# Decoder kernel in fp32: K and V products in three reduced-precision passes, a new order of the side work, and an output projection begun in the last head group

## Chip, cores and metric

The kernel runs on one core of a Trainium2 chip. The metric is device time in microseconds (us), median of several runs; lower is better.

## What is computed

There are three residual blocks on `x` of shape (16, 224, 512), each behind a layer norm; all arrays are float32. Cut to what matters:

```python
# 1 mixer: Q, K, products with V_b, W_b, ..., a running sum over the 224 tokens, @ Wo.T
# 2 attention over ctx (16, 750, 256), 16 heads of 32
Q  = (ln(x) @ Wq.T).reshape(B, 224, 16, 32)
KV = (ctx @ Wkv.T).reshape(B, 750, 2, 16, 32)       # Wkv is (1024, 256)
x  = x + softmax(Q K^T * 32**-0.5) V @ Wo.T
# 3 router and 32 experts
probs  = softmax(ln(x) @ gate_w.T + gate_b, over the tokens)
vals, idx = top 8 tokens of each expert
merged = sum_k vals[k] * ln(x)[idx[k]]              # one row of 512 per batch and expert
o = gelu([merged, 1] @ w1[e]) ...; o = [h, 1] @ w2[e]   # w1, w2: 256 MB in all
x = x + scatter of o * vals
```

## The kernel before

**Stages.** A setup loads and transposes the weights. A main stage does mixer, attention and router of the 16 batch elements in turn. A last stage runs all 32 experts, whose 128 weight chunks of 2 MB stream through `ring`, eight slots of SBUF; it ends with the scatter. The first eight chunks are loaded during the last batch element, into space that the main stage no longer needs (`first_weights`, L647).

**Main stage.** The 16 heads are four groups `kt` of four. TensorE makes the scores twice. `scores` (L1261, matmul at L1272) makes them with the queries on partitions, only to get each query's maximum: 16 matmuls of 375 columns a group into banks 2 to 4, each reduced by VectorE (`take_max`, L1072). `join_maxima` (L1079), a transpose on TensorE (`turn_max`, L1279), `max_rows` on VectorE (L1089, L1092) and two DMAs of ScalarE's queue (`stack_max`, L906) put the negated maxima into two rows of `q_st`. Then `scores_T` (L1282, matmul at L1294) makes the scores with the keys on partitions, with the maxima subtracted, in 12 units of 2x224 columns; ScalarE takes `exp` of each (L886). `values` (L1311) multiplies with V a third of the keys at a time; GpSimd sums the probabilities (`sum_keys`, L760 to L767, 896 columns an instruction), `denominators` (L1322) sums that over partitions, and `normalise` on VectorE (L1100 to L1108) divides. The maxima of group n+1 are made during group n.

**Precision.** Both kinds of scores are made of float32r operands, split into a high and a low part that stand under each other on the partitions (`k_hi`, `k_lo`, `q_hi`, `q_lo`, stacked by 24 DMAs a group on SyncE's queue). All other matmuls, those for K (L1223), V (L1230) and the output projection (L1236) among them, are float32.

**The order of the work** is written out by hand. A group has 16 steps. Each engine walks through the same steps: in step 1 to 12 one unit of `scores_T` and its `exp`; in `PV_AT` the first two `values`, in step 1 of the next group the third; `MAXIMA` says how many maxima each step makes for the next group; `TURN_AT` the step of `join_maxima`, with the transpose and the rows one step later. `TIMETABLE` lays the other products ("jobs", function `fill` on each engine) of the next and of the past batch element into the steps: `ct0` to `ct3` transpose the context, `k0.0` to `k3.1` and `v0` to `v5` make K and V, `q0` to `q3` Q, `xt`, `pz`, `pc`, `pa`, `mix` the mixer, `yt` the transposed input of attention, `out0`, `out1` the output projection of the past element, `rt`, `gate`, `wt`, `merge`, `mt` the router. A job writes bank 0 or 1, in turn, and waits until the job two before it is read out. `AT` places the norms and the parts of the router's softmax. SyncE loads `x` and the context of the next element at the start of a batch element (`load_x`) and behind the first stack (`load_ctx`), and ScalarE may overwrite `k_hi` when the last stack of K has been copied out.

**The tail.** Behind the last group come the last `values`, `denominators`, `normalise`, `out0`, `out1`, the store of `x2`, the router's jobs, and then the barrier ahead of the experts. `mt` (L1044) writes the merged rows into `merged_T`, which is held from the start with one column for each element.

## Time and profile before

| | |
|---|---|
| median of 3 runs | 2317.16 us (2315.62 to 2319.82) |
| the profiled execution | 2323.09 us, its span 2321.4 us |
| granted TensorE clock, mean | 0.919 |
| busy in the span | TensorE 83%, VectorE 42%, GpSimd 36%, ScalarE 32% |
| transfers of the whole | 419.34 MB |

The span falls into setup (to 43.5 us), a prologue that fills the pipeline (to about 105 us), 16 batch elements (to about 1607 us), the tail (to 1640 us) and the experts with the scatter. In the rows an instruction's "mean ns" goes from its start to its modelled end; matmuls overlap, so the distance from one start to the next is shorter. A float32 matmul of the code is two records.

### The profile page before, as it was taken

To read this page: it belongs to the slowest core of one execution; us is meant where nothing else is said; L and a number is where in the kernel's file an instruction comes from. 1 tells how busy PE (TensorE), PEld (TensorE's weight loads), DVE (VectorE), ACT (ScalarE), POOL (GpSimd) and SP (SyncE) were. 2 spreads that over 40 slices of the span, in tenths; PEclk is the share of its full clock that TensorE was granted. 3 is DMA by queue.
4 is the path that set the end of the run, shared out by engine and by line. 5 is a ranking of instruction groups with operands and counts; after the bars stand their busy time and mean duration, and the time that the engine had idled before them with its cause. 6 is when DMAs were issued, how large, how long until landed. Compare 5 with 4: busy or idle time off the path is not lost. (4 is left out here: it accounts for less than half of the span.)

```text
span 2321.4 us, 40341 instructions
## 1 busy us (share of the span) xinstructions
PE 1931.5 (83%) x12130; PEld 1138.9 (49%) x12130; DVE 974.4 (42%) x2473; ACT 748.8 (32%) x1551; POOL 827.3 (36%) x592
## 2 busy tenths in 40 slices
PE   7789999999999999999999999997665556655544
PEld 5466666666666666666666666653211111111111
DVE  1355655656656556565565665653100000000003
ACT  3243444435444344344443544432100000000000
POOL 0255554545555455555455555544000000000000
PEclk9999999999999999999999999997877777777777
DMA  6224223243242332423324223255699999999996
GB/s 179 71 68 105 61 75 90 74 102 71 68 98 76 87 86 68 97 70 78 89 74 104 66 71 95 76 169 203 247 419 422 420 420 421 421 421 421 421 377 244
DMA packets 139167, 419.34 MB, mean 181 GB/s; under 512 B 32780, under 2 KB 74988, under 8 KB 114556
## 3 DMA queue, kind: packets, MB, share of 16 engines
q1 hardware_dynamic: 131484, 409.73, 51.8%
q10 hardware_dynamic: 6656, 8.15, 1.0%
q0 software_dynamic: 992, 1.02, 0.1%
q8 instruction: 19, 0.31, 0.1%
q14 instruction: 16, 0.13, 0.0%
HBM read 306.39 MB, written 16.15 MB: 139 GB/s over the span
## 5 line engine op out<-in xcount | busy, mean ns | idle before, releaser
L1072 DVE TENSOR_REDUCE maxes<-bank 112x1 f32<-112x376 f32 (+1 forms) x1024 | 506.7, 538 | 204.7 <-PE bank L1272 203.9
L886 ACT ACTIVATE probs<-bank 125x448 f32<-125x448 f32 x768 | 402.7, 547 | 369.0 <-PE bank L1294 362.4
L1294 PE MATMUL bank<-q_st,k_st 98*125 98x224 f32 x1536 | 384.0, 339 | 21.5 <-DMA q_st<-max_lo 10.3
L764 POOL TENSOR_TENSOR psum_keys<-psum_keys,probs 125x896 f32<-125x896 f32 x128 | 269.1, 2102 | 327.8 <-ACT probs L886 322.2
L1656 PE MATMUL bank<-ring,hid_T 128*32 128x512 f32 x1024 | 177.9, 857 | 199.7 <-DMA ring<-in_L_ffn_w 196.4
L1272 PE MATMUL bank<-k_st,q_st 96*112 96x376 f32 (+1 forms) x1024 | 324.0, 367 | 13.2 <-DVE maxes L1072 7.6
L1294 PEld LDWEIGHTS bank<-q_st,k_st 98*125 98x125 f32 x1536 | 265.2, 192 | 132.2 <-issue 68.8
L767 POOL TENSOR_TENSOR psum_keys<-psum_keys,probs 125x896 f32<-125x896 f32 x128 | 267.7, 2092 | 10.0
L1574 DVE TENSOR_TENSOR o_fin<-bank,b_row 16x512 f32<-16x512 f32 x32 | 21.7, 679 | 589.3 <-PE bank L1614 589.3
L1497 POOL DMA_DIRECT2D o_rows<-o_fin x31 | 15.3, 493 | 598.1 <-DVE o_fin L1574 598.1
L1629 PE MATMUL bank<-ring,tok 128*32 128x512 f32 x1024 | 145.2, 693 | 76.4 <-DMA ring<-in_L_ffn_w 74.3
L1272 PEld LDWEIGHTS bank<-k_st,q_st 96*112 96x112 f32 x1024 | 164.4, 179 | 77.6 <-DVE maxes L1072 46.8
L1656 PEld LDWEIGHTS bank<-ring,hid_T 128*32 128x32 f32 x1024 | 45.0, 150 | 308.2 <-issue 302.4
L1311 PE MATMUL bank<-probs,v 125*32 125x224 f32 x3072 | 190.1, 366 | 2.2 <-ACT probs L886 2.2
L1223 PE MATMUL bank<-ctx_T,wk_T 128*128 128x376 f32 (+1 forms) x512 | 183.2, 485 | 3.5 <-DVE q_lo L1025 2.6
L1230 PE MATMUL bank<-wv_T,ctx_T 128*125 128x512 f32 x384 | 183.4, 607 | 0.9 <-DVE q_lo L1025 0.9
L760 POOL TENSOR_TENSOR psum_keys<-probs 125x896 f32<-125x896 f32 x64 | 134.2, 2098 | 129.3 <-ACT probs L886 120.0
L1031 DVE TENSOR_TENSOR k_lo<-bank,k_hi 128x376 fp32r<-128x376 f32 (+1 forms) x128 | 69.8, 546 | 131.7 <-ACT k_hi L828 126.3
L1522 ACT COPY o_sb<-bank 128x512 f32<-128x512 f32 x32 | 18.7, 586 | 326.5 <-PE bank L1656 326.5
L724 POOL TENSOR_TENSOR rstd<-mean_var,small 112x2 f32<-112x2 f32 x48 | 9.4, 195 | 304.7 <-DVE mean_var L967 301.2
L1629 PEld LDWEIGHTS bank<-ring,tok 128*32 128x32 f32 x1024 | 33.0, 118 | 172.4 <-DMA ring<-in_L_ffn_w 103.3
L1236 PE MATMUL bank<-wo_T,o_T 128*112 128x512 f32 x256 | 115.9, 606 | 1.7 <-DVE o_T L1108 1.7
(149 smaller groups left out, 2268.6 us busy)
## 6 DMA issues: line engine op xcount, KB each, us to landing
ring<-in_L_ffn_w SPq DMA_DIRECT2D x128, 2048.0 KB, 30.5
k_st<-k_hi SPq DMA_DIRECT2D x512, 93.8 KB, 2.2
k_st<-k_lo SPq DMA_DIRECT2D x256, 93.8 KB, 2.2
q_st<-q_hi SPq DMA_DIRECT2D x504, 28.0 KB, 1.8
ctx_nat<-in_ctx SPq DMA_DIRECT2D x16, 750.0 KB
x_in<-in_x SPq DMA_DIRECT2D x16, 448.0 KB, 3.6
out<-x SPq DMA_DIRECT2D x16, 448.0 KB, 8.1
out<-ring ACTq DMA_DIRECT2D x28, 256.0 KB, 3.1
```

The source lines that it names most:

```text
L760: nc.gpsimd.tensor_tensor(psum_keys[:], lo, hi, ALU.add).then_inc(keys_summed, 1)
L764: nc.gpsimd.tensor_tensor(psum_keys[:], psum_keys[:], lo, ALU.add).then_inc(pool_chain, 1)
L767: nc.gpsimd.tensor_tensor(psum_keys[:], psum_keys[:], hi, ALU.add).then_inc(keys_summed, 1)
L886: nc.scalar.activation(probs[n % 2][:, j, :], bank[5 + u % 2][0:SK, 0:2 * T], ACT.Exp, scale=SCALE).then_inc(probs_ready, 1)
L1072: nc.vector.tensor_reduce(maxes[:, j, t, c:c + 1], bank[2 + n % 3][0:TT, 0:SC[c + 1] - SC[c]], AX.X, ALU.max).then_inc(s_drained, 1)
L1223: last = nc.tensor.matmul(ps[:, 0:SC[c + 1] - SC[c]], wk_T[:, kc, kt * P:(kt + 1) * P], ctx_T[:, kc, chunk(c)], start=(kc == 0), stop=(kc ...
L1230: last = nc.tensor.matmul(ps[0:SK, :], ctx_T[:, kc, i * SK:(i + 1) * SK], wv_T[:, kc, :], start=(kc == 0), stop=(kc == KC - 1))
L1272: nc.tensor.matmul(bank[2 + n % 3][0:TT, 0:SC[c + 1] - SC[c]], q_st[slot][0:3 * HD, j, t * TT:(t + 1) * TT], k_st[slot][0:3 * HD, j, chunk ...
L1294: last = nc.tensor.matmul(bank[5 + u % 2][0:SK, kk * T:(kk + 1) * T], k_st[slot][:, j, k * SK:(k + 1) * SK], q_st[slot][:, j, :], start=Tr ...
L1311: last = nc.tensor.matmul(bank[7][j * HD:(j + 1) * HD, 0:T], v[:, 2 * c + kk, col:col + HD], p[:, j, kk * T:(kk + 1) * T], start=(c == 0 a ...
L1629: last = nc.tensor.matmul(bank[e2][c * 32:(c + 1) * 32, :], tok[:, e2, kd, :], ring[:, slot, col:col + BANK], start=(kd == 0), stop=(kd == ...
L1656: last = nc.tensor.matmul(bank[5 + e2][c * 32:(c + 1) * 32, :], hid_T[:, e2, t, c * 32:(c + 1) * 32], ring[:, slot, col:col + D], start=(t ...
```

## The change

1. **K and V.** The weights `wk`, `wv` and the transposed context are split into float32r high and low parts: the weights once in the setup (four VectorE subtractions), the context in each `ct` job (ScalarE writes `ctx_hi`, VectorE then subtracts into `ctx_lo`). Each float32 product becomes three: high x high, high x low, low x high.
2. **All steps are laid anew**: `TIMETABLE`, `MAXIMA`, `AT`, `PV_AT`, `SUM_AT`, and `TURN_AT` goes from 11 to 13. The transposed maxima go to bank 4, which the third matmul of the next maxima uses, and the wait on `max_ready` moves from the first to the third.
3. **Loads** of `x` and context are issued one batch element earlier.
4. **Memory.** `v` shares its space with `merged_T` and the experts' first biases. So `mt` writes a small `m_now`, which is stored to DRAM for each element (`keep_routed`) and read back in the tail behind the last `values` (`recall_routed`), together with the biases.
5. **Last group of the last element.** `begin_out` puts the products of three of the four groups of `out0` and `out1` at steps 7 and 11; in the tail only the fourth is left. The last two sums of keys on GpSimd are left out, and TensorE sums that third of the keys itself (`last_denominators`).

```diff
 TIMETABLE = (
+    [(0, s, j) for s, j in ((1, "v4"), (2, "v5"), (2, "q3"), (4, "k3.0"), (5, "k3.1"),
+                              (6, "xt0"), (7, "xt1"), (8, "out0"), (9, "ct0"), (11, "out1"),
+                              (11, "ct1"), (13, "pz"), (14, "pc"), (15, "pa"))]
+    + [(1, s, j) for s, j in ((1, "ct2"), (2, "mix0"), (2, "ct3"), (4, "mix1"), (5, "k0.0"),
+                              (8, "yt0"), (9, "yt1"), (11, "q0"))]
+    + [(2, s, j) for s, j in ((0, "k0.1"), (1, "rt0"), (2, "rt1"), (5, "gate"), (10, "q1"),
+                              (12, "wt0"), (12, "wt1"), (13, "merge"))]
+    + [(3, s, j) for s, j in ((0, "k1.0"), (1, "k1.1"), (2, "mt"), (5, "q2"), (7, "v0"),
+                              (9, "v1"), (10, "k2.0"), (11, "k2.1"), (13, "v2"), (14, "v3"))]
+BEGIN_OUT = {(3, 7): "out0", (3, 11): "out1"}
-PV_AT = {6: 0, 10: 1}
+PV_AT = {6: 0, 12: 1}
-SUM_AT = {6: 0, 10: 1, 14: 2}
-TURN_AT = 11
+SUM_AT = {5: 0, 11: 1, 14: 2}
+TURN_AT = 13
-MAXIMA = ((3, 0, 3, 0, 0, 2, 2, 1, 2, 2, 1),
-          (0, 2, 1, 0, 2, 1, 3, 2, 2, 2, 1),
-          (3, 2, 0, 0, 0, 2, 2, 2, 1, 2, 2),
-          (1, 3, 1, 0, 2, 3, 0, 0, 2, 2, 2))
+MAXIMA = ((3, 3, 3, 1, 2, 2, 0, 0, 0, 1, 1),
+          (0, 1, 0, 0, 0, 3, 1, 3, 1, 2, 1, 2, 2),
+          (1, 2, 1, 0, 2, 2, 0, 2, 2, 0, 1, 1, 2),
+          (4, 0, 1, 0, 1, 2, 1, 1, 0, 2, 1, 2, 1))
...
+                def recall_routed():
+
+                    sp.wait_ge(pv_done, 12 * B)
+                    expert_biases()
+                    sp.wait_ge(m_stored, 16 * B)
+                    sp.dma_start(merged_T[:, 0:LAST].rearrange("p b k e -> p b (k e)"),
+                                 routed[0:LAST].rearrange("b p n -> p b n")
+                                 ).then_inc(routed_loaded, 16)
...
+                    elif job[:2] == "ct":
+                        kc, cols = i % 2, slice(i // 2 * 3 * SK, (i // 2 + 1) * 3 * SK)
+                        dve.wait_ge(work_full, full)
+                        dve.wait_ge(ctx_hi_ready, bb * 4 + (i + 1))
+                        nc.vector.tensor_tensor(ctx_lo[:, kc, cols], ps[:, 0:3 * SK],
+                                                ctx_hi[:, kc, cols].bitcast(F32), ALU.subtract
+                                                ).then_inc(s, 1)
...
+                        terms = [(ctx_hi, wv_hi), (ctx_hi, wv_lo), (ctx_lo, wv_hi)]
                         for kc in range(KC):
-                            last = nc.tensor.matmul(ps[0:SK, :], ctx_T[:, kc, i * SK:(i + 1) * SK],
-                                                    wv_T[:, kc, :], start=(kc == 0),
-                                                    stop=(kc == KC - 1))
+                            for n, (z, w) in enumerate(terms):
+                                last = nc.tensor.matmul(ps[0:SK, :],
+                                                        z[:, kc, i * SK:(i + 1) * SK], w[:, kc, :],
+                                                        start=(kc == 0 and n == 0),
+                                                        stop=(kc == KC - 1 and n == 2))
...
+                def last_denominators():
+
+                    p = probs[(3 * G - 1) % 2]
+                    pe.wait_ge(keys_summed, B * 12 - 1)
+                    for n in range(3):
+                        for j in range(4):
+                            part = p[:, j, (n - 1) * T:n * T] if n else psum_keys[:, j, :]
+                            last = nc.tensor.matmul(bank[7][j * HD:(j + 1) * HD, T:2 * T],
+                                                    ones[0:SK, 0:HD], part,
+                                                    start=(n == 0), stop=(n == 2))
+                    last.then_inc(den_done, 1)
+
+                def begin_out(job):
+
+                    wait_out(pe, *before(job, "tail", LAST + 1))
+                    pe.wait_ge(o_ready, LAST * 4 + (G - 1))
+                    for kt in range(G - 1):
+                        nc.tensor.matmul(bank_of(job, "tail")[0:TT, :],
+                                         tokens(o_T[:, kt, :], OUT[job][2]), wo_T[:, kt, :],
+                                         start=(kt == 0), stop=False)
```

The old `TIMETABLE` stands at L32 to L43. K's product (L1219 to L1226) is changed as V's is, with weight and context in each other's place.

## Rows read from the trace of the kernel before

**Rows 1.** The page: TensorE's busy tenths in 40 slices of 58 us
```profile
PE   7789999999999999999999999997665556655544
```
**Rows 2.** Busy time by stretch: main loop, last element, tail, experts (after POOL: clock, DMA share)
```profile
300.00:1500.00 1200.00, 1167.99 (x7662) 781.52 (x7660) 715.54 (x1799) 536.62 (x1133) 634.48 (x435) 1.00 0.33 81
1500.00:1600.00 100.00, 86.91 (x570) 53.66 (x570) 48.68 (x119) 38.47 (x82) 51.37 (x28) 0.88 0.57 194
1600.00:1640.00 40.00, 23.74 (x108) 11.39 (x105) 6.10 (x18) 7.58 (x17) 9.68 (x9) 0.67 0.22 79
1640.00:2321.00 681.00, 391.51 (x2324) 114.37 (x2324) 72.08 (x225) 57.84 (x97) 16.81 (x33) 0.78 0.97 396
```
**Rows 3.** Line 606, the context's loads: duration min/median/max, first and last start
```profile
L606 SPq DMA_DIRECT2D ctx_nat<-in_ctx x15: 285/301/482, 129.1 to 1455.0; - x15
```
**Rows 4.** Timeline of TensorE (start, us first start to last end), and single durations
```profile
L1230 PE MATMUL bank<-wv_T,ctx_T x384: 590/592/1216, 66.8 to 1529.7; 128*125 128x512 f32 x192
L1223 PE MATMUL bank<-ctx_T,wk_T x512: 475/478/611, 46.1 to 1535.8; 128*128 128x376 f32 x86, 128*128 128x374 f32 x85
...
1007.78 2.69 PE L1223 MATMUL bank<-ctx_T,wk_T 128*128 128x376 f32 x8
...
1048.47 3.60 PE L1230 MATMUL bank<-wv_T,ctx_T 128*125 128x512 f32 x8
```
**Rows 5.** The same for the float32r matmuls of both kinds of scores
```profile
L1272 PE MATMUL bank<-k_st,q_st x1024: 326/336/784, 88.2 to 1585.3; 96*112 96x376 f32 x171
...
L1294 PE MATMUL bank<-q_st,k_st x1536: 263/273/1174, 103.7 to 1605.0; 98*125 98x224 f32 x192
...
1004.07 0.51 PE L1272 MATMUL bank<-k_st,q_st 96*112 96x376 f32 x2
1004.42 0.38 PE L1294 MATMUL bank<-q_st,k_st 98*125 98x224 f32 x2
```
**Rows 6.** Groups by line: busy us, mean ns, idle before and releaser
```profile
L1072 DVE TENSOR_REDUCE maxes<-bank 112x1 f32<-112x376 f32 (+1 forms) x1024 | 506.7, 538 | 204.7 <-PE bank L1272 203.9
L1031 DVE TENSOR_TENSOR k_lo<-bank,k_hi 128x376 fp32r<-128x376 f32 (+1 forms) x128 | 69.8, 546 | 131.7 <-ACT k_hi L828 126.3 <-PE bank L1223 4.0
L828 ACT CAST k_hi<-bank 128x376 fp32r<-128x376 f32 (+1 forms) x128 | 60.4, 472 | 137.5 <-DMA k_st<-k_hi 82.7 <-PE bank L1223 50.5 <-issue 4.3
```
**Rows 7.** Timeline of all engines, from the transposed maxima to the next group's first unit
```profile
1027.17 0.26 PE L1279 MATMUL bank<-ident,q_max 112*8 112x112 f32 x1 [0.28 <-DVE q_max L1079]
...
1028.98 0.63 ACTq L906 DMA_DIRECT2D q_st<-max_lo  x1
...
1031.01 0.47 PE L1294 MATMUL bank<-q_st,k_st 98*125 98x224 f32 x2
...
1031.58 0.52 SPq L627 DMA_DIRECT2D k_st<-k_hi  x1
...
1041.72 0.48 PE L1294 MATMUL bank<-q_st,k_st 98*125 98x224 f32 x2 [0.21 <-ACT probs L886]
```
**Rows 8.** Timeline of TensorE, last groups and tail, with idle time before and releaser
```profile
1586.82 0.26 PE L1279 MATMUL bank<-ident,q_max 112*8 112x112 f32 x1
...
1593.51 1.18 PE L1294 MATMUL bank<-q_st,k_st 98*125 98x224 f32 x4 [3.52 <-DMA q_st<-max_lo]
...
1610.62 0.97 PE L1322 MATMUL bank<-psum_keys,ones 125*32 125x224 f32 x8 [2.79 <-POOL psum_keys L767]
1613.34 8.96 PE L1236 MATMUL bank<-wo_T,o_T 128*112 128x512 f32 x16 [1.74 <-DVE o_T L1108]
```
**Rows 9.** The chain that ended last, an expert pair's wait; and a group of DMA issues
```profile
1869.25 34.88 DMA ring<-in_L_ffn_w
...
x_in<-in_x SPq DMA_DIRECT2D x16, 448.0 KB, 3.6
```
**Rows 10.** Timeline of SyncE's queue in the tail
```profile
1594.31 11.49 SPq L430 DMA_DIRECT2D ring<-in_L_ffn_w  x2
1623.05 0.35 SPq L640 DMA_DIRECT2D out<-x  x1
```

More of the change, by code:

```diff
@@ L679, in step @@
                             store(b - 1)
+                        if kt == 1 and not (isint(b) and b + 2 > LAST):
+                            load_ctx(b + 2)
+                        if kt == 2 and not (isint(b) and b + 2 > LAST):
+                            load_x(b + 2)
                         if kt == 0:
@@ L683, in step @@
                             stack(b + 1, kt - 1)
[L684 to L685 removed]
                         if kt == 3 and kind != "first":
                             keep_weight(b - 1)
+                        if kt == 3 and kind != "first":
+                            keep_routed(b - 1)
                         if kind == "last" and kt == 1:
[L689 removed]
                             sp.wait_ge(x1_ready, 2 * B)
@@ L701, in step @@
                             first_weights([2 + kt])
-                batches(sp, step)
+                step("pro", -1)
+                step("first", 0)
+                with sp.Fori(1, LAST - 1) as b:
+                    step("mid", b)
+                step("mid", LAST - 1)
+                step("last", LAST)
+                step("tail", LAST + 1)
                 sp.wait_ge(x2_stored, 16 * B)
@@ L791, in step @@
                                 root(2, norm_no(2, kind, b))
-                            if s in SUM_AT:
+                            if s in SUM_AT and not (kind == "last" and (kt, SUM_AT[s]) == (3, 2)):
                                 sum_keys(b, kt, SUM_AT[s])
@@ L1176, in fill @@
                     prev = before(job, kind, b)
-                    if prev:
+                    if prev and not (kind == "tail" and job[:3] == "out"):
                         wait_out(pe, *prev)
@@ L1368, in step @@
                                     denominators(b - 1, G - 1)
+                            if kind == "last" and (kt, s) in BEGIN_OUT:
+                                begin_out(BEGIN_OUT[kt, s])
                             if s in PV_AT:
```

134 lines of the change are left out of this document (81 added, 53 removed).

## The prediction

> **What bounds the kernel now.** I first read the page's slices [rows 1]: from the 4th to the 27th of 40 TensorE's digit is 9. The table by stretch [rows 2] makes it exact: from 300 to 1500 us TensorE is busy 1168 of 1200 us at a granted clock of 1.00 (2.4 GHz), VectorE 716, GpSimd 634, ScalarE 537, DMA 0.33. So the loop over the batch elements is bound by TensorE, and since the clock is already full there, it has nothing to give back. One element takes (1455.0 - 129.1) / 14 = 94.7 us [rows 3]. The last element (clock 0.88) and the tail (0.67) are looser: there TensorE waits in a chain. From 1640 us the DMA share is 0.97, and the chain that ended last is made of waits of some 35 us for expert weights [rows 2, 9]. That stage is as long as its transfers take and starts behind a barrier, so what the stages ahead of it save arrives at the end one for one. The change doesn't touch its transfers.
>
> **K and V, the main term.** In a run of n records of one matmul, (length - one duration) / (n - 1) is the distance from start to start. V's 512 columns: (3.60 - 0.59) / 7 = 0.430 us; K's 376: (2.69 - 0.48) / 7 = 0.316 us [rows 4]. Both are 0.84 ns a column, twice the 0.42 ns of a 2.4 GHz column, so a float32 record is two passes and a float32 matmul four. The float32r scores: 0.51 - 0.336 = 0.173 us for 376 columns, 0.38 - 0.27 = 0.107 for 224 [rows 5]: one pass (0.157, 0.093) and some 15 ns. The weights loaded there have 112 and 125 columns, K's have 128 and V's 125, so I take the same 15 ns. A `k` job goes from 4 x 0.316 = 1.26 to 6 x 0.173 = 1.04 us; 8 x 16 jobs save 29 us. A `v` job goes from 4 x 0.430 = 1.72 to 6 x (0.215 + 0.015) = 1.38; 6 x 16 jobs save 33 us. Together **-61.5 us** of TensorE time, 3.8 us an element.
>
> The Trainium skill ("TensorE: Matmul & The Clock Gate", section "Back-to-back issue gap") puts the distance of warm matmuls at N/2.4 + 2.5 ns. By that estimate a pass of 376 columns takes 0.159 us and one of 512 takes 0.216, and the two terms would be 40 and 41 us, 81 in all. The rows of this trace (0.173 for 376) say otherwise, and my sum goes by them.
>
> **What is paid for it.** Each `ct` job gets a VectorE subtraction like k_lo's, 0.55 us [rows 6]: 64 in all, 2.2 us an element. VectorE goes from 716 / 1200 x 94.7 = 56.5 to 58.7 us an element, against some 91 of TensorE. In the sum it costs nothing, as long as TensorE has other jobs between `ct3` at (1, 2) and `k0.0` at (1, 5); it has `mix1`. In the setup four subtractions stand behind the last copies and in the prologue K waits for both halves of the context: +1.5 us (0 to 3).
>
> **The new order** moves nearly every job, and the trace can't show how its waits fall. I walk through the seams of the groups with the durations above. (a) Group 1 to 2. The maxima are transposed in step 14 instead of 12, and steps 13 and 15 are empty. In the trace the first unit of the next group starts 3.84 us after the transpose (1027.17 to 1031.01), without waiting for the DMA; the second DMA's issue ends at 2.44 us [rows 7]. So the chain is 2.4 to 3.8 us. In the new order it is covered by `k0.1` 1.04, a third `values` 0.9, two maxima 0.35 and `rt0` 0.4 = 2.7: a stall of 0 to 1.1, I take 1.1, as the landing of a DMA has never been seen under 1 us. (b) The transpose itself waits for the last reductions: two maxima stand in step 12 with only `values` behind them, and each reduction takes 0.54 us [rows 6]: 0 to 1.2, I take 0.5. (c) Group 2 to 3: covered by 3.6 us, 0.2 left. (d) `mix0`, three steps earlier, comes 1.7 us behind `pa`, whose four VectorE operations take about 2: 0.3. (e) The first six steps of group 0 now hold 14 maxima instead of 8, 7.5 us of reductions beside other VectorE work, against some 12 us of TensorE work: 0 to 1.5, I take 0.3. Sum 2.4 us an element.
>
> Against it: ScalarE waited 82.7 us for the stacks of K to be copied out before it could overwrite `k_hi` [rows 6], about 2.6 us twice an element, and its `exp` queued behind. At 1041.72 a unit of TensorE starts some 0.7 us late, released by ScalarE [rows 7]. The reason is that SyncE was still sending `q1`'s stack: the stack behind `k1.1` began at 1031.58, some 4 us after its job [rows 7]. Now `q1` stands seven steps ahead of `k1.1` instead of three, 16 steps lie between `k0.1` and `k1.0`, and nine full ones (some 12 us for 12 DMAs of 0.6 us) between `k1.1` and `k2.0`. Both waits should go: -1.2. The maxima's bank 4 takes away the wait of the next maxima for `max_lo`: -0.2. Net +1.0 us an element, times 15: **+15 us**; the bounds are -1.4 (no new stall) and +4.5 (every upper end, no relief), so -21 to +67.
>
> **SyncE's queue.** `x` and context come an element earlier; each load stands behind a wait that the jobs have passed by then (`ct3` and `mix1`), and the stacks behind it are due from step 11 of the same group, so nothing waits. `keep_routed` adds one DMA of 64 KB an element: 0, beside a queue with room; without that cover its issue, about 0.35 us.
>
> **Last element.** Its groups are short of jobs, and weights fill the DMA queues: from the transpose to the next unit 1593.51 - 1586.82 = 6.7 us, 3.5 of them idle [rows 8]. Transposing later makes that up to 1 us longer in three groups: **+2** (0 to 4).
>
> **Tail.** Before: 16 records of the projection in 8.96 us, 0.56 each, as the clock is low. Twelve leave the tail: -6.7. The wait of 2.8 us for GpSimd goes [rows 8]. Sixteen more records of `denominators` cost twice 0.97: +2.0. The twelve records come into the last group at 0.43 (full clock) to 0.86 (half): +5.2 to +10.3, less about 1 us of waits they fill. Sum -3.3 to +1.8, I take **-1**. `recall_routed` puts five DMAs ahead of the store of `x2`, behind the last `values` at about 1608, and the store comes at 1623.05 [rows 10]. 960 KB at the pace of `x_in` (448 KB in 3.6 us) take 8 us [rows 9], behind a weight chunk issued near 1606. They are through by about 1620: 0, and up to +4 if they are slower.
>
> **The sum:** -61.5 + 15 + 1.5 + 2 - 1 = -44 us. The profiled execution took 2323.1 us and would take 2279. It lies 5.9 above the median shown, which would go from 2317.2 to **2273**.
>
> **The rivals.**
> *All of it arrives, and more.* The new order has no new stall and old ones go too: -61.5 - 21 + 3 = up to -80, typically -65: 2252. For it: TensorE's busy time hides late units like that at 1041.72, and its open idle time is 32 us of 1200 [rows 2], so an order can close more than the seams cost. Against: the seams above. By the skill's formula the same time would come out by shorter passes, 2317 - 81 + 17 = 2253; rows 5 speak against that. Chance 0.17.
> *Much is given back.* VectorE, with 2.2 us more and the maxima crowded into the first steps, paces TensorE through reductions and late subtractions; stalls of 3 us an element net: -61.5 + 45 + 2 = -14: 2303. For it: `maxes` is the costliest VectorE group [rows 6], and the third maximum on always waits for one of its three banks. Chance 0.18.
> *Slower.* The chain maximum, transpose, rows, two DMAs ends every group and not one of four. Its price is what it lacks of cover at each seam; from (61.5 - 2.5) / 15 = 3.9 us an element, about 1 us at each of four seams, the gain is gone, and at 1.3 us each it is +19: 2336. For it: TURN_AT is two steps later in all groups. Against: groups 0 and 3 have `pc`, `pa` (6 us) and `v3`, `v4` behind the transpose. Chance 0.03.
> *The passes aren't short:* a float32r record with 128 weight columns costs as a float32 one. Then K and V grow by half, 2 x 128 x 0.316 + 2 x 96 x 0.430 = +163 us. Rows 5 exclude it nearly; I put under 0.01 on it, within the slower case.
>
> **How the numbers follow.** Forecast 0.62 (2260 to 2292), more 0.17, given back 0.18, slower 0.03. The range 2249 to 2301 leaves out the tail of the second case (0.08) and of the third (0.08), and the slower one. A measurement of this kernel can tell about 0.2%, 4.6 us, from no change. Faster by more 0.95, within 0.02, slower 0.03.
>
> **What would show it.** K and V: 6 records a job, 0.17 and 0.23 us from start to start, 768 and 576 records where there were 512 and 384. The period by the context's loads: 91.9 us instead of 94.7. Idle time of TensorE released by `max_lo`'s DMA, or a unit late behind the transpose, in the first steps of group 2. ScalarE's wait for `k_hi`'s DMA near 0. In the tail a projection of four records and no wait for GpSimd. The experts' stage still 681 us. I'm wrong if the period stays above 94, or if the passes are 0.16 or shorter.

## The result, and the profile after

| | before | after |
|---|---|---|
| median | 2318.01 us | 2259.64 us (4 runs, 2251.44 to 2262.85) |
| the profiled execution | 2323.09 us, span 2321.4 | 2257.76 us, span 2256.1 |
| granted TensorE clock, mean | 0.919 | 0.912 |

The ratio of the two is 0.974, with an interval of 0.9724 to 0.9755: 58 us less by the medians, 65.3 by the spans. 2273 was forecast, in a range of 2249 to 2301.

I cut both spans at the same events. "First unit" is the first matmul of `scores_T` (L1294 before, L1367 after) of group 0 of a batch element; elements count from 0.

| us from the span's start | before | after | what the stretch gained (-) or lost (+) |
|---|---|---|---|
| first unit of element 0 | 103.7 | 111.2 | setup and prologue +7.5 |
| of element 1 | 200.2 | 200.7 | -7.0 |
| of element 2 | 298.4 | 290.8 | -8.1 |
| of element 14 | 1433.1 | 1370.9 | 12 elements, -54.6: 94.56 to 90.01 us each |
| of element 15, the last | 1527.7 | 1460.8 | -4.7 |
| last unit | 1605.0 | 1549.7 | last element +11.6 |
| first matmul of the experts | 1643.0 | 1580.3 | tail -7.4 |
| end | 2321.4 | 2256.1 | experts -2.6 |

The page of after, TensorE's busy tenths and its granted clock in 40 slices of 56 us (compare [rows 1]):
```profile
PE   7889999999999999999999999976756656556544
PEclk9799999999999999999999999977878787787776
```
The clock's second digit, 7, is the prologue. Next is the table by stretch of after, columns as in [rows 2]: main loop, last element, tail, experts.
```profile
300.00:1360.00 1060.00, 1022.22 (x7437) 768.07 (x7437) 699.02 (x1706) 493.36 (x1049) 589.28 (x401) 1.00 0.34 87
1460.80:1549.70 88.90, 71.90 (x425) 45.95 (x424) 36.02 (x85) 30.43 (x63) 39.91 (x23) 0.75 0.55 200
1549.70:1580.30 30.60, 13.06 (x102) 6.77 (x101) 8.81 (x23) 5.19 (x12) 3.73 (x7) 0.74 0.43 132
1580.30:2256.00 675.70, 391.71 (x2320) 114.89 (x2320) 69.89 (x219) 57.84 (x97) 15.24 (x31) 0.78 0.98 399
```
And two stretches of before that were not shown, the same part of the loop and the last element:
```profile
300.00:1360.00 1060.00, 1031.68 (x6751) 688.31 (x6750) 629.05 (x1579) 472.37 (x997) 559.14 (x382) 1.00 0.33 81
1527.70:1605.00 77.30, 65.09 (x425) 41.02 (x423) 34.89 (x86) 29.74 (x62) 39.77 (x23) 0.81 0.60 222
```
The loop is bound by TensorE at full clock in both; the experts' stage stayed as long as its transfers (DMA 0.98). The last element lost time, with more idle time (17.0 us instead of 12.2) and a lower clock.

Context loads of after, by line (compare [rows 3]; the move ahead of each load in the loop is the row to take, as the first loads stand in the prologue): (1315.0 - 235.0) / 12 = 90.0 us an element.
```profile
L635 SPq MOVE ctx_nat<-in_ctx x13: 29/29/29, 235.0 to 1315.0; - x13
```
Timeline of TensorE, single records of V and K (compare [rows 4]):
```profile
1459.35 0.40 PE L1302 MATMUL bank<-wv_hi,ctx_hi 128*125 128x512 f32 x1
1459.58 0.40 PE L1302 MATMUL bank<-wv_lo,ctx_hi 128*125 128x512 f32 x1
...
1466.41 0.34 PE L1292 MATMUL bank<-ctx_hi,wk_hi 128*128 128x376 f32 x1
...
1467.27 0.34 PE L1292 MATMUL bank<-ctx_hi,wk_lo 128*128 128x376 f32 x1
```
V's records start 0.23 us apart (0.234 over a job of six), K's (1467.27 - 1466.41) / 5 = 0.172.

Group by line of after (compare [rows 6]), ScalarE's write of `k_hi`:
```profile
L885 ACT CAST k_hi<-bank 128x376 fp32r<-128x376 f32 (+1 forms) x128 | 60.1, 470 | 135.5 <-PE bank L1292 127.7 <-issue 4.3 <-DMA k_st<-k_hi 3.0
```
ScalarE's wait for `k_hi` to be copied out went from 82.7 us [rows 6] to 3.0.

The tail of after, from the timelines of TensorE, SyncE and ScalarE (compare [rows 8, 10]):
```profile
1554.42 1.98 PE L1309 MATMUL bank<-wo_T,o_T 128*112 128x512 f32 x4 [1.64 <-DVE o_T L1175]
...
1557.16 1.59 SPq L669 DMA_DIRECT2D out<-x  x1
...
1563.52 1.52 ACT L904 ACTIVATE x<-x,shift,rstd 112x512 f32<-112x512 f32 x2 [12.89 <-DMA out<-x]
```
The projection is four records, and nothing waits for GpSimd. But the stored `x2` is used 6.4 us after its store is issued; before, the store at 1623.05 [rows 10] was used at 1626.18, after 3.1.

### The profile page after: what moved, and what is told of

It is laid out like the page before. It is cut to its first block and busy times, and to the rows that moved or that the text cites. A ratio compares the mean times of both kernels' runs of the same rounds, so it can differ in the third digit from the quotient of the medians.

```text
span 2256.1 us, 41492 instructions
## 1 busy us (share of the span) xinstructions
PE 1858.3 (82%) x12594; PEld 1211.7 (54%) x12594; DVE 1028.3 (46%) x2541; ACT 745.9 (33%) x1551; POOL 823.6 (37%) x591
## 5 line engine op out<-in xcount | busy, mean ns | idle before, releaser
L1367 PE MATMUL bank<-q_st,k_st 98*125 98x224 f32 x1536 | 338.6, 307 | 23.5 <-DMA q_st<-max_lo 21.9
L1367 PEld LDWEIGHTS bank<-q_st,k_st 98*125 98x125 f32 x1536 | 258.3, 192 | 82.2 <-issue 48.1
L1345 PEld LDWEIGHTS bank<-k_st,q_st 96*112 96x112 f32 x1024 | 170.2, 181 | 77.9 <-DVE maxes L1139 50.3
L1384 PE MATMUL bank<-probs,late 125*32 125x224 f32 x3072 | 188.7, 364 | 0.0
L1283 PE MATMUL bank<-yT,wq_T 128*128 128x224 f32 x512 | 112.2, 364 | 4.0 <-DVE k_lo L1088 3.2
L1384 PEld LDWEIGHTS bank<-probs,late 125*32 125x32 f32 x3072 | 81.1, 110 | 57.9 <-issue 21.5
L1309 PE MATMUL bank<-wo_T,o_T 128*112 128x512 f32 x244 | 109.9, 593 | 1.6 <-DVE o_T L1175 1.6
L889 ACT COPY late<-bank 125x512 f32<-125x512 f32 x96 | 56.2, 586 | 159.7 <-PE bank L1302 159.7
## 6 DMA issues: line engine op xcount, KB each, us to landing
k_st<-k_hi SPq DMA_DIRECT2D x512, 93.8 KB, 2.1
k_st<-k_lo SPq DMA_DIRECT2D x256, 93.8 KB, 2.2
```

Source lines behind the costliest of these rows:

```text
L1283: last = nc.tensor.matmul(ps[:, 0:T], wq_T[:, kd, i * P:(i + 1) * P], yT[:, kd, :], start=(kd == 0), stop=(kd == KD - 1))
L1309: last = nc.tensor.matmul(ps[0:TT, :], tokens(o_T[:, kt, :], i), wo_T[:, kt, :], start=(kt == 0), stop=(kt == G - 1))
L1345: nc.tensor.matmul(score_bank(n)[0:TT, 0:SC[c + 1] - SC[c]], q_st[slot][0:3 * HD, j, t * TT:(t + 1) * TT], k_st[slot][0:3 * HD, j, chunk(c ...
L1367: last = nc.tensor.matmul(bank[5 + u % 2][0:SK, kk * T:(kk + 1) * T], k_st[slot][:, j, k * SK:(k + 1) * SK], q_st[slot][:, j, :], start=Tr ...
L1384: last = nc.tensor.matmul(bank[7][j * HD:(j + 1) * HD, 0:T], v[:, 2 * c + kk, col:col + HD], p[:, j, kk * T:(kk + 1) * T], start=(c == 0 a ...
```

## The experiments

### 1. The long products in the new order

```diff
-                            for n, (w, z) in enumerate(terms):
+                            for w, z in terms[0:1]:
...
-                                                        w[:, kc, kt * P:(kt + 1) * P],
-                                                        z[:, kc, chunk(c)],
+                                                        w[:, kc, kt * P:(kt + 1) * P].bitcast(F32),
+                                                        z[:, kc, chunk(c)].bitcast(F32),
```
(V's product likewise.)

> The changed kernel with its order, splits and tail, but K and V are one float32 product each again (high x high, four passes; the low parts are left out of the result, VectorE still makes them). Theory 1, the loop runs at TensorE's pace and the passes and the order add: the element's period goes from 90.0 to 90.0 + 8 x (1.26 - 1.03) + 6 x (1.72 - 1.40) = 93.8 us, the time to about 2318. Rival, the saved time came mostly from the new order and its seams have room for the longer products: at most 92.5 us and 2298.

Measured: 2304.18 us (median of 4), ratio to the kernel before 0.994 (0.9923 to 0.9956), span 2301.6, loop 92.96 us an element at clock 1.00. That lies between the theory (93.8) and the rival (92.5 or less). So the loop's 94.56 to 90.01 splits into two parts. The new order with all that comes with it, VectorE's subtractions too, is worth -1.60 us an element, though +1.0 was forecast. The short passes are worth 92.96 - 90.01 = 2.95 of their 3.75. By groups 0 to 3, from first unit to first unit, an element takes 30.9, 21.9, 17.9 and 23.8 us before, 30.9, 21.2, 18.5 and 22.4 in this run, and 30.2, 21.3, 18.3 and 20.3 after: most of both gains lies in group 3.

Where the lost 0.8 goes is seen in TensorE's groups from 300 to 1360 us, in the last columns (idle time, releaser). First before, then this run, then after; in each the upper row is `scores_T`, the lower `scores`:
```profile
L1294 PE MATMUL bank<-q_st,k_st 98*125 98x224 f32 x1074 | 266.6, 335 | 6.6 <-ACT probs L886 5.2
L1272 PE MATMUL bank<-k_st,q_st 96*112 96x376 f32 x716 | 222.3, 361 | 8.4 <-DVE maxes L1072 4.8 <-DVE max_lo L1092 2.0
```
```profile
L1368 PE MATMUL bank<-q_st,k_st 98*125 98x224 f32 x1092 | 265.4, 328 | 3.2 <-DMA q_st<-max_lo 3.2
L1346 PE MATMUL bank<-k_st,q_st 96*112 96x374 f32 x722 | 228.8, 362 | 8.7 <-DVE maxes L1139 7.8
```
```profile
L1367 PE MATMUL bank<-q_st,k_st 98*125 98x224 f32 x1136 | 246.1, 302 | 6.7 <-DMA q_st<-max_lo 6.7
L1345 PE MATMUL bank<-k_st,q_st 96*112 96x376 f32 x750 | 229.9, 352 | 11.5 <-DVE maxes L1139 10.6
```
The waits for `probs` and `max_lo` on VectorE are gone with the new order. With the short passes on top, the maxima's DMA and VectorE's reductions are waited for longer: summed over all its groups, TensorE's idle time in the stretch is 28.4 us before, 29.8 in this run and 37.7 after, so the short passes add 7.9 / 11.8 elements = 0.7 us an element. The rows shown don't hold all waits: beside them the new order has a new one, of `wt0` for ScalarE and VectorE, 10.7 us in this run and 11.7 after, and the old waits for GpSimd's sums (6.5 us) and for `xh` (3.1) are gone.

### 2. The short products in the old order

The tables, `PV_AT`, `SUM_AT`, `AT` and `MAXIMA` of before and `TURN_AT = 11`, in the changed kernel.

> The changed kernel with short passes, memory plan and tail, but the tables of before (TIMETABLE, MAXIMA, AT, PV_AT, SUM_AT, TURN_AT). Theory 1: period 94.6 - 3.75 = 90.9 us, total about 12 us above the changed kernel. Rival, the old order can't use shorter passes (its ends wait for VectorE and for the stacks' DMAs): 92.4 us or more, total 2295 or more. Second rival, my forecast's own term, the new order costs +1.0 an element: then the old order would be the faster one, 89.0.

Measured: 2359.75 us, ratio 1.018 (1.0159 to 1.0201), 97.58 us an element, group 1 now 25.9 us where it was 21.9. It is the first rival's case (92.4 or more, 2295 or more), and well beyond it. With the order of before, the short passes and the subtractions that come with them make the kernel slower. The timeline of TensorE at the `ct` jobs, and the busy table of the stretches around it (the granted clock is the last number but two):
```profile
440.86 0.89 PE L1264 MATMUL bank<-ident,ctx_nat 125*128 125x125 f32 x3 [2.26 <-DVE ctx_lo L1112]
```
```profile
437.00:440.60 3.60, 1.60 (x11) 1.08 (x9) 3.35 (x10) 1.49 (x3) 0.53 (x3) 1.00 0.00 0
440.60:444.00 3.40, 3.14 (x18) 2.51 (x22) 2.37 (x6) 2.05 (x4) 2.81 (x3) 0.50 0.00 0
444.00:447.50 3.50, 3.50 (x25) 2.47 (x15) 1.30 (x4) 1.79 (x4) 0.00 (x0) 0.51 0.00 0
447.50:451.00 3.50, 3.50 (x37) 2.88 (x36) 2.94 (x8) 3.10 (x6) 1.96 (x1) 1.00 0.19 55
```
The old order puts `ct0`, `ct1` and `ct2` into one step. Each now holds its bank until VectorE has subtracted, so TensorE idles 2.26 us; and behind that wait its clock is granted at 0.50, 1.2 GHz, until 447.5. The wait of 2.26 us is followed by half clock in every element of the stretch. For 75.1 us of the 1060 the clock was at half, with TensorE busy for 73.1 of them; half of that is lost, some 3.4 us an element beside the waits.

### 3. The old order with its `ct` jobs spread

As run 2, but `ct0` and `ct1` go from step 5 of group 1 to steps 12 and 13 of group 0.

> As b_old (short passes, the tables of before), with ct0 and ct1 moved from step 5 of group 1 to steps 12 and 13 of group 0. In b_old TensorE waits 2.3 us for ctx_lo between the ct jobs and its granted clock is 0.5 for the next 7 us, in every element. Theory 2 (one wait of about 2 us costs twice, as the clock falls behind it): with the wait gone both go, 2.3 and about 3 us: period from 97.6 to 92 or less. Rival, VectorE's extra work itself is what costs 3 us in the old order: it stays above 95. Second rival, only the wait is gained and the clock falls elsewhere: about 95.

Measured: 2334.17 us, ratio 1.0071 (1.0056 to 1.0087), 95.56 us an element at clock 0.99, where 92 or less was expected with both the wait and the clock won: theory 2 fell. 2.0 us an element came back, and all of it is busy time (half clock in only 17.1 us of the stretch, instead of 75.1). The wait at `ct` went, but as much idle time stands in other places, some 6.3 us an element in both runs. TensorE's groups in the same stretch show where:
```profile
L1367 PE MATMUL bank<-q_st,k_st 98*125 98x224 f32 x1062 | 231.5, 304 | 26.1 <-ACT probs L943 17.1 <-DMA q_st<-max_lo 9.0
L1345 PE MATMUL bank<-k_st,q_st 96*112 96x376 f32 x710 | 217.7, 355 | 22.7 <-DVE maxes L1139 21.2
```
In all TensorE idles 70.1 us there, 3.8 us an element more than before. The short passes save 3.75, so the sum is about 94.6. Of the 0.9 left the trace gives most to the clock: in five of the 11 elements it still falls to half, in all for 17.1 us in which TensorE is busy throughout, so half of that, 0.8 us an element, is lost. In the old order what is taken from K and V comes back as waits.

### 4. Two records more, taken away

The third of the three products is left out of each K and V product (low weight x high context for K, low context x high weight for V).

> Low x high is left out of K and V, so two passes instead of three; everything else as changed. Theory 1: the period falls by TensorE's whole saving, 16 x 0.172 + 12 x 0.234 = 5.6 us, to 84.4. Rival, VectorE or the chain of the maxima is close behind and takes over: 87 or more.

Measured in a single execution: 2259.57 us, 89.73 us an element, where after has 90.01, for 28 records less, 5.6 us of TensorE work: the rival (87 or more). Group 3 is 2.1 us shorter, but group 0 is 2.3 longer. The reason is in TensorE's timeline and the busy table:
```profile
478.61 1.00 PE L1257 MATMUL bank<-ident,xh 112*128 112x112 f32 x4 [1.65 <-DVE k_lo L1088]
```
```profile
478.30:485.10 6.80, 6.50 (x31) 3.91 (x32) 1.98 (x5) 2.79 (x7) 4.44 (x2) 0.50 0.19 45
```
`xt0` takes the bank of `k3.0` and waits for VectorE to read it out, and behind the wait the clock is at half. The wait is the same in every element (1.62 to 1.66 us), yet the clock falls behind it in seven of twelve only. Elements without the fall take 88.4 us, those with it 90 to 91.5. So the change's order has almost nothing more to give for still shorter K and V jobs.

### 5. More work for VectorE

```diff
+                        dve.wait_ge(spared, bb * 4 + i)
+                        nc.vector.tensor_reduce(spare[:], ps[:, 0:3 * SK], AX.X,
+                                                ALU.max).then_inc(spared, 1)
```
In each `ct` job one reduction more, ahead of the subtraction, whose result nobody reads.

> Each ct job has one more VectorE instruction of 0.54 us (a maximum over the same 375 columns, thrown away), 2.2 us an element. Theory 1, VectorE's work is hidden: the period grows by 0 to 0.4 us. Rival, VectorE paces the loop in these steps: by 1 to 2.2 us.

Measured in a single execution: 2264.63 us, 90.33 us an element, +0.3, for 4 x 0.55 = 2.2 us of VectorE time, as theory 1 says. The change's own four subtractions are of the same size and in the same place, so they should cost no more; a run without them was not made. Beside run 2 this says that it isn't VectorE's total that stands in the way, but what one matmul waits for in one place.

### 6. The transpose one step earlier

`TURN_AT = 12`, and the maxima of groups 1 to 3 that stood in step 12 moved into step 11.

> The changed kernel with TURN_AT 12 instead of 13 and the maxima of step 12 put into step 11 in groups 1 to 3. If the seam into group 2 costs a stall of about 1 us as I forecast (3.7 us from the transpose to the next unit, with 2.7 us of work in it), an earlier transpose gives up to 1 us an element, 15 us. Rival, the seam only moves the wait: the transpose then waits for VectorE, and the period stays within 0.3 us of 90.0.

Measured: 2271.49 us, ratio 0.98 (0.9785 to 0.9815), 90.92 us an element, +0.9. From transpose to next unit it is 3.72 us into group 2, as in after (3.71), and 5.14 into group 3 instead of 3.91. TensorE's waits for `maxes` go from 10.6 to 17.1 us, as four maxima in one step wait for the reductions of the first ones. Neither the gain nor the rival's "within 0.3 us" came. The prediction's seam (a) exists, but 13 is the better place for it than 12 in this order.

### 7. The end of the last group as before

`BEGIN_OUT` is empty, the sums of keys stay on GpSimd and `denominators` closes the last group.

> The changed kernel without its fifth part: both output products whole in the tail, the sums of keys on GpSimd back, the last denominators as before. My forecast for that part was -3.3 to +1.8 us, I took -1: so this kernel 1 us slower than the changed one, from last unit to the experts' first matmul 9 us longer, and the last group 4 to 8 us shorter. Rival, the part is worth 5 us or more, as the records in the last group fill waits.

Measured: 2262.14 us, ratio 0.9751 (0.9732 to 0.977), span 2259.6. The medians are 2.5 apart and the intervals overlap; the trace tells more. The last unit comes 6.2 us earlier (1543.5), since the twelve records are gone from the group, and the experts 2.9 later (1583.2):
```profile
1550.47 0.59 PE L1395 MATMUL bank<-psum_keys,ones 125*32 125x224 f32 x8 [3.39 <-POOL psum_keys L824]
...
1552.79 9.55 PE L1309 MATMUL bank<-wo_T,o_T 128*112 128x512 f32 x16 [1.74 <-DVE o_T L1175]
```
Part 5 costs 6.2 us in the group, as estimated, saves 9.1 behind it, and so is worth some 3.

### 8. TensorE kept busy in prologue and tail

```diff
+                FILL = {("pro", "ct2"): 3, ("pro", "k0.0"): 3, ("pro", "xt0"): 5,
+                        ("pro", "pz"): 2, ("pro", "yt0"): 7, ("pro", "q0"): 2, ("pro", "q1"): 8,
+                        ("tail", "rt0"): 20, ("tail", "gate"): 2, ("tail", "wt0"): 7}
...
+                    spare = FILL.get((kind, job), 0)
+                    for _ in range(spare):
+                        nc.tensor.matmul(bank[6][:, 0:T], ident[:], ones[:], start=True, stop=True)
```
Thrown-away matmuls of 224 columns where TensorE only waits, and five more ahead of the experts.

> The changed kernel with spare matmuls (ident x ones, 0.19 us a record at full clock, into bank 6, which nobody reads then) in TensorE's waits of the prologue and the tail and ahead of the first expert: 3 to 8 ahead of ct2, k0.0, xt0, pz, yt0, q0, q1, 20 ahead of the tail's rt0, 2 and 7 ahead of gate and wt0, 5 ahead of the first expert. Nothing else moves. Theory 2: the prologue's clock rises from 0.77 to above 0.9 and the first unit of scores comes 5 to 8 us earlier, the tail's gate and the first expert run at full clock, 3 to 4 us: 8 to 11 us in all. Rival, the clock isn't what those stretches wait for: 0, or slower by the spare matmuls.

Measured: 2250.99 us (median of 5), ratio 0.971 (0.9697 to 0.9723). In the prologue the first unit comes at 104.2, 7.0 us earlier than in after. In runs 7, 9 and 10, whose prologue is after's, it came at 111.3, 113.3 and 112.9, and in run 11, with the same spare matmuls, at 104.0: the step is larger than the scatter. The busy table of the prologue to the first unit, before, after and this run:
```profile
43.50:103.70 60.20, 47.05 (x163) 30.68 (x164) 21.50 (x48) 12.56 (x25) 15.34 (x14) 0.91 0.31 73
```
```profile
43.50:111.20 67.70, 52.31 (x188) 41.01 (x189) 23.99 (x53) 12.76 (x25) 15.48 (x15) 0.77 0.30 74
```
```profile
43.50:104.20 60.70, 54.15 (x248) 43.39 (x248) 24.68 (x55) 13.25 (x26) 15.50 (x15) 0.94 0.32 78
```
The same work with 60 records more, and 7.0 us faster, at a clock of 0.94 instead of 0.77. The clock is the larger part of the prologue's loss: of 7.5 us between before and after 5.3 are busy time (47.05 to 52.31), 2.2 idle time. In after it begins with two waits of TensorE, for the new subtractions, behind which K's records stand 0.31 us apart, nearly twice the 0.172 of the loop:
```profile
45.67 1.51 PE L1264 MATMUL bank<-ident,ctx_nat 125*128 125x125 f32 x6 [1.18 <-DVE ctx_lo L1112]
...
48.48 0.65 PE L1292 MATMUL bank<-ctx_hi,wk_hi 128*128 128x376 f32 x1 [1.30 <-DVE ctx_lo L1112]
...
48.93 0.52 PE L1292 MATMUL bank<-ctx_lo,wk_hi 128*128 128x376 f32 x1
```
In the tail the full clock (1.00 from 1550 to 1580) brought 1.4 us only, of the 3 to 4 expected there and at the first expert. The likely reason, for which no run was made, is that the chain there runs through the other engines.

### 9. The store of `x2` ahead of the read-back

`recall_routed` goes behind `store`.

> The changed kernel with recall_routed (four DMAs of biases and merged rows) behind the store of x2 instead of ahead of it. In the changed kernel 6.4 us lie between the issue of that store (1557.16) and ScalarE's first use of the stored rows (1563.52); before the change it was 3.1. Theory 1: the store stands behind recall_routed's transfers in the DMA engines; without them the 6.4 fall to about 3, the experts start 3 us earlier and the time is 3 us less than that of the changed kernel (about 2256.5), as the read-back is needed only by the experts. Theory 2: slot 7's weight chunk, issued at 1550.37, is what the store stands behind; then 1 us at most is won. Theory 3: the biases and merged rows now come late for the experts and the time is the same or longer.

Measured: 2257.84 us, ratio 0.9741 (0.9725 to 0.9756), which by the medians can't be told from after. The trace can: timeline of SyncE and ScalarE,
```profile
1556.53 0.35 SPq L669 DMA_DIRECT2D out<-x  x1
...
1559.79 1.52 ACT L904 ACTIVATE x<-x,shift,rstd 112x512 f32<-112x512 f32 x2 [9.79 <-DMA out<-x]
```
3.3 us instead of 6.4, and the experts begin 27.5 us behind the last unit instead of 30.6, with the same stage behind them (675.9). Theory 1, by the trace. The whole span is 3.6 us shorter than after's: the first unit came 2.1 us later, the last element, which the edit doesn't touch, took 2.7 less (86.2 us), and 3.1 were won behind it. Against scatter of that size the medians, 1.8 us apart, don't tell.

### 10. The last element's weight chunks later

```diff
-                            first_weights([0])
...
-                            first_weights([1, 2])
+                            sp.wait_ge(scores_ready, (LAST * 4 + 1) * 12 + 1)
+                            first_weights([0, 1])
...
+                            sp.wait_ge(scores_ready, (LAST * 4 + 2) * 12 + 1)
+                            first_weights([2, 3, 4])
```
(and slots 5 and 6 behind the first unit of group 3.)

> The changed kernel with the last batch element's weight chunks issued later: slots 0 and 1 behind the first unit of group 1, slots 2 to 4 behind the first unit of group 2, slots 5 and 6 behind the first unit of group 3, so that none is issued shortly ahead of the two DMAs of the maxima. In the changed kernel four chunks were issued at 1483.1 to 1486.8 and TensorE then idled 6.55 us until 1489.82 for the maxima's DMA, and 4.56 us at the next seam. Theory 1: the small DMA stands behind the chunks in the DMA engines; the two seams fall to about 2.2 us of idle time, the last element is 6 us shorter and so is the time (about 2253.5). Theory 2: the chunks lie beside any seam, whenever they are issued; the loss moves to other seams and the time stays within 2 us. Theory 3: the chunks are late for the experts, whose stage starts with waits for them: the stage is longer by what the last element wins, or more.

Measured: 2248.55 us, ratio 0.9698 (0.9683 to 0.9714), span 2244.5. To read it, see the seam into group 1 of the last element in after, timeline of all engines, behind the transpose at 1481.76. The two DMAs of ScalarE's queue carry the maxima:
```profile
1482.65 0.64 ACTq L963 DMA_DIRECT2D q_st<-max_hi  x1
...
1483.11 1.43 SPq L444 DMA_DIRECT2D ring<-in_L_ffn_w  x2
1483.32 0.84 ACTq L963 DMA_DIRECT2D q_st<-max_lo  x1
...
1489.82 1.18 PE L1367 MATMUL bank<-q_st,k_st 98*125 98x224 f32 x4 [6.55 <-DMA q_st<-max_lo]
```
and the same seam before, where four loads of biases and then the first chunk stand in SyncE's queue:
```profile
1550.23 2.26 SPq L654 DMA_DIRECT2D b_rows<-in_L_ffn_w  x4
1550.68 0.63 ACTq L906 DMA_DIRECT2D q_st<-max_lo  x1
1552.53 0.90 SPq L424 DMA_DIRECT2D ring<-in_L_ffn_w  x2
...
1553.95 0.76 PE L1294 MATMUL bank<-q_st,k_st 98*125 98x224 f32 x2 [2.40 <-DMA q_st<-max_lo]
```
Then this run:
```profile
1484.63 0.63 ACTq L962 DMA_DIRECT2D q_st<-max_lo  x1
...
1487.38 0.93 PE L1366 MATMUL bank<-q_st,k_st 98*125 98x224 f32 x4 [2.79 <-DMA q_st<-max_lo]
1487.99 0.85 SPq L444 DMA_DIRECT2D ring<-in_L_ffn_w  x2
```
In after the first chunk of 2 MB goes out while `max_hi` is being issued, ahead of `max_lo`, and the unit starts 5.7 us after `max_lo`'s issue ended (1484.16); here it is 2.1. Before, the bias loads kept the chunks back by 2.3 us, past `max_lo`; the change moved them into `recall_routed`. But that is only half of the cause. Run 2 has lost the bias loads too, with the old tables, and there the same seam is nearly free:
```profile
1593.90 0.63 ACTq L963 DMA_DIRECT2D q_st<-max_lo  x1
1594.90 1.48 SPq L444 DMA_DIRECT2D ring<-in_L_ffn_w  x2
...
1596.08 0.48 PE L1367 MATMUL bank<-q_st,k_st 98*125 98x224 f32 x2 [1.32 <-DMA q_st<-max_lo]
```
The issue of `max_lo` ends 22.4 us after the element's first unit there, in after 23.4 us, and so it is just ahead of the chunk. In run 3 it ends at 22.4 too; the chunk comes in the middle of it, and the unit 2.9 us behind its end. The last element takes 77.4 and 78.9 us in these two runs, the twelve records of part 5 included. So the collision needs both, the bias loads gone and the later maxima of the new order. `TURN_AT` alone doesn't decide it: in run 6, with 12, the chunk still meets the maxima and TensorE waits 7.75 us.

In run 10, over the last element, TensorE's waits for `max_lo` fall from 13.3 us to 5.4, the clock rises from 0.75 to 0.86, and the element takes 75.3 us instead of 88.9. Theory 1 expected 6; the gain between these two executions is 13.6, as 6.8 us of it are busy time (71.9 to 65.1), at the higher clock. How much of that the edit causes isn't sure, as the clock of this stretch varies. With after's order of chunks the last element took 88.9, 88.7 (run 8), 88.5 (run 5) and 86.2 us (run 9), and in run 6 83.3 us at a clock of 0.84, though its waits for `max_lo` are as long (14.9 us). With the later chunks it took 75.3 and 77.0 (run 11). The medians of the whole are 11.1 us apart. The edit moves the chunks of all three seams at once, and the waits fall at each: 6.55 to 2.79 us, 4.56 to 1.18, 2.18 to 1.43. The experts' stage is unchanged (676.0), so theory 3 falls too.

### 11. All three edits

> The two edits of this call together with the thrown-away matmuls of the run that kept TensorE's clock up in the prologue and the tail: meant to be faster than both kernels. If all add up: -8 (thrown-away matmuls, measured by medians), -3 (store ahead of the read-back), -6 (later chunks) against the changed kernel's 2259.6: 2243. If the waits removed overlap, the last element's clock or the experts' first transfers take some back: 2247. At or above 2251, the thrown-away matmuls' own time, the two other edits are worth nothing together.

Measured: 2238.60 us (median of 5, 2237.84 to 2242.95), ratio 0.9658 (0.9644 to 0.9672), 21.0 us below the changed kernel and 80 below the one before. It is faster than the 2243 expected because run 10 was worth more than 6; by the medians of runs 8, 9 and 10, 8.7 + 1.8 + 11.1 = 21.6 us, the three add up. First unit at 104.0, loop 90.01, last element 76.9, last unit to experts 26.9 (30.6 in after). It is the best version of this study.

### 12. Q's jobs earlier in the kernel before

```diff
-    + [(2, s, j) for s, j in ((0, "rt0"), (1, "rt1"), (3, "gate"), (8, "q1"), (10, "k1.0"),
+    + [(2, s, j) for s, j in ((0, "rt0"), (1, "rt1"), (3, "gate"), (5, "q1"), (10, "k1.0"),
...
-    + [(3, s, j) for s, j in ((1, "merge"), (4, "mt"), (5, "q2"), (7, "k2.0"), (9, "k2.1"),
+    + [(3, s, j) for s, j in ((1, "merge"), (2, "mt"), (3, "q2"), (7, "k2.0"), (9, "k2.1"),
```

> The kernel before, whole, but for its table: q1 goes from step 8 to 5 of group 2, q2 from step 5 to 3 of group 3 (mt from 4 to 2 with it), so that SyncE has sent Q's stack before K's stack is due. In the kernel before ScalarE waits 56.9 us in the stretch 300 to 1360 for the stacks of K to be copied out of k_hi, 5 us an element. Theory 1 (the prediction's step): this wait falls by more than half and the element gets about 1.2 us shorter, the time 18 us less (ratio 0.992). Theory 2: the wait is hidden behind other work of TensorE; it falls, but the period stays within 0.3 us of 94.56 (ratio 0.998 to 1.002), and the gain of the new order came from elsewhere.

Measured: 2342.04 us, ratio 1.0103 (1.0087 to 1.0119), 95.79 us an element: neither theory. ScalarE's wait for `k_hi`, 56.9 us in the stretch, is halved:
```profile
L828 ACT CAST k_hi<-bank 128x376 fp32r<-128x376 f32 x88 | 41.5, 471 | 85.9 <-PE bank L1223 58.0 <-DMA k_st<-k_hi 27.9
```
and a late unit behind `k2.1` goes: job and unit start 0.97 us apart instead of 1.65. But `q2` at step 3 puts its subtraction on VectorE together with `normalise`, and five maxima queue behind them:
```profile
757.79 0.39 DVE L1108 TENSOR_TENSOR o_T<-bank,o_T 128x224 f32<-128x224 f32 x1
758.09 2.35 DVE L1072 TENSOR_REDUCE maxes<-bank 112x1 f32<-112x374 f32 x5
758.69 0.88 PE L1272 MATMUL bank<-k_st,q_st 96*112 96x376 f32 x2 [1.39 <-DVE maxes L1072]
```
This comes in every element (TensorE's waits for `maxes` go from 4.8 to 20.0 us, 1.4 an element). Behind it the clock fell to half in two of the eleven elements, which makes at most 0.5 of the 1.2 us an element lost. So ScalarE's wait did cost time, 0.7 us an element by the distance from job to unit, and the collision that came with one job moved by two steps costs more.

## Why the prediction was right, and which steps failed

**What held.** TensorE bounds the loop at full clock, and the experts start earlier by what is saved ahead of them. The passes: K 0.173 forecast, 0.172 measured; V 0.230 and 0.234. With 768 and 576 records, 512 x 0.316 - 768 x 0.172 = 29.7 us and 384 x 0.430 - 576 x 0.234 = 30.3, 60.0 of the 61.5 forecast. By the trace, then, a record costs its pass and some 15 to 21 ns. The rule that the prediction weighed (the Trainium skill, "TensorE: Matmul & The Clock Gate", section "Back-to-back issue gap": N/2.4 + 2.5 ns, which the page calls the gap of isolated matmuls) gives 0.159 and 0.216; as a price for this kernel's records the trace is against it, by 13 and 18 ns a record. ScalarE's wait for `k_hi` vanished. VectorE's subtractions are nearly hidden in the loop, as far as run 5 can show it. Part 5 costs in the group what was estimated. Two slips of the working changed nothing: TensorE's time an element is 1168 / 1200 x 94.7 = 92.2 us and not 91, and the upper ends of the stalls add up to 4.3 us and not 4.5.

**The new order, "+1.0 us an element", failed.** Four stalls were listed at 2.4 us and two reliefs at 1.4. Run 1 gives -1.6 for the order as a whole. By TensorE's idle time, sorted by group over elements 2 to 13, the stalls that exist are: (a) 0.56 us an element for `max_lo`'s DMA in group 2, against 1.1, and run 6 shows that it can't be bought off with an earlier transpose; (b) 0.65 for the last reductions, in group 1, against 0.5. (c) and (d) did not come. Nor did (e): group 0, with its 14 early maxima, has no wait for `maxes`. They stand in group 1, 0.88 us, of which 0.43 were there before. And one stall was not on the list at all: `wt0` in group 2 waits 0.98 us for ScalarE's `weight` and for its bank. What is new in this adds up to 2.6 us, near the 2.4 of the forecast, but it is made of other parts, and the agreement is luck. What was missed is on the other side. Old waits of 1.5 us an element went, for GpSimd's sums, `probs`, `xh` and `max_lo` on VectorE, so that the idle time of before and of run 1 is nearly the same (28.4 and 29.8 us), and the period falls by 1.6 beyond that. What the old order lost was therefore not idle time in the groups' rows but late units inside "busy" time, like the one at 1041.72 [rows 7]. I had read one of them and priced the kind at 1.2; from the start of each record to the start of the next, units, maxima, K, V and `ct` together take 53.1 us an element before and 50.5 in run 1 (the units alone 18.6 and 16.8), with the same records; all other kinds take 1.0 more.

**The passes' return was mis-sized the other way.** I let all 3.8 us an element arrive. 2.95 did; 0.7 came back as idle time, most of it waits for the maxima. Together: forecast -3.8 + 1.0 = -2.8 us an element, measured -4.55. That is the rival "all of it arrives, and more" in the loop, which had -65 in all; over elements 0 to 14 the time fell by 74.4 us, the first two giving 15.1 of it.

**Setup and prologue, "+1.5 us (0 to 3)", failed: +7.5.** I counted the subtractions, and they cost about 2.5 us of waits. What I left out is the clock behind them: 0.91 before, 0.77 after, and with it go 5.3 us of longer busy time. Run 8 gives the 7 us back without touching the subtractions.

**The last element, "+2 (0 to 4)", failed: +11.6.** 6.2 of it are the twelve records (run 7), which the prediction booked under the tail. The other 5.4 against 2 forecast are the weight chunks that came ahead of the maxima's DMA, and the lower clock that went with the waits. The step that failed is "Last element": I looked at the transpose's place, and not at the queue from which the four bias loads had gone. Their cover of 2.3 us had kept the chunks behind the seam, and with the maxima about 1 us later than the old tables have them with the same passes, the first chunk met them (run 10, beside runs 2 and 3). Run 10 gives back 13.6 us in its execution and 11.1 by the medians.

**Tail, "-1 (-3.3 to +1.8)", with recall "0, up to +4".** Part 5 is worth about -3 (run 7), the read-back costs +3 (run 9). Both lie in the bounds, and they cancel.

**The sum.** By the table: +7.5 - 74.4 + 11.6 - 7.4 - 2.6 = -65.3, where -44 was forecast. The median fell by 58 and lies at 2259.6, just below the likeliest case (2260 to 2292) and above the rival's 2252: the loop did what the rival says, and the prologue and the last element gave some 9 us of it back (6 and 3 above their forecasts). That the range held is owed in part to errors of opposite sign.

**The other rivals.** "Much is given back" fell for this order; but in the old order its mechanism is there, waits for reductions and late subtractions, and takes more than that case had: run 3 gives all of the passes' gain back and is 16 us slower than before. Run 2 is slower still, through a place I had not named (`ct0` to `ct2` in one step). The rival "the passes aren't short" fell with the records above.

**What stays open.** Which moves of the new order brought the 1.6 us isn't settled: by groups they lie in 1 and 3, and run 12 separates one of them and finds a gain of 0.7 under a loss. The experts' stage came out 2.6 us shorter; over all executions shown here it took 674.6 to 678.6 us, so this may be scatter.

## What to carry to other kernels

When a product gets shorter in an order written out by hand, its gain may only be had with a new order: here the short passes came with +16 us or more in the two versions of the old one, against the kernel before, and with -45 in the new one, against the long passes there. Price an order by the distances from start to start of the units, not by idle time. And when small loads leave a queue, ask what was standing behind them: 2 MB chunks issued within a microsecond of a transfer of a few KB on which TensorE waits cost some 11 us here by the medians, and these were had back by waiting for the first unit of the group.

## What the runs showed of the hardware

- Behind a wait of 2.26 us in an otherwise full loop (run 2) the clock was granted at 0.50, 1.2 GHz, in every element of the stretch. Behind one of 1.62 to 1.66 us (run 4) this happened in seven of twelve elements, behind one of 1.39 us (run 12) in two of eleven. In run 2's rows at half clock TensorE is busy for 6.6 us, so about 3.3 us are lost there beside the wait itself.
- Thrown-away matmuls in waits made the prologue 7.0 us shorter, at a granted clock of 0.94 instead of 0.77 (run 8).
- The two rows of the maxima, a transfer of a few KB, took 2.1 us from the end of its issue to the unit that waits for it with no chunk near (run 10), 1.6 with one issued 0.4 us behind it (run 2), 2.9 with one issued during its issue (run 3), and 5.7 with 2 MB chunks issued from just ahead of it on (after). A store of 448 KB was used 3.3 us after its issue, and 6.4 behind the read-back.
